# GpSimd makes the first tap of three convolved tiles and the rounding step of softplus; VectorE goes on from its results

## The chip, the core and the metric

The kernel runs on one core of a Trainium2 chip. The metric is the device time of one execution in microseconds (us); lower is better. The core has a matrix engine (TensorE, PE), VectorE (DVE), ScalarE (ACT), GpSimd (POOL) and SyncE (SP), which here only issues DMAs. Each engine runs its instructions in order, and semaphores order them between engines.

## What is computed

The reference normalises x (4 batches of 1024 tokens, 256 features), runs a stack of 8 Mamba layers on it, runs a mixture of experts on the same normalised input, and joins the two. The Mamba stack is where nearly all of the time goes. One layer, cut to what matters:

```
xin, z = split(x @ Wi.T)                          # 512 channels each
xin    = silu(causal_conv(xin, cw, cb))           # 4 taps a channel, plus a bias
dt_raw, Bm, Cm = split(xin @ Wx.T)                # 16, 16, 16
delta  = softplus(dt_raw @ Wdt.T + bdt)
h      = h * exp(delta * A) + (delta * xin) * Bm  # one h for each channel and each of 16 states
y      = sum over states of h * Cm, plus xin * Dp
x      = x + (y * silu(z)) @ Wo.T
```

## The kernel before

A *unit* is one layer, one batch and one half of its 1024 tokens: T = 512 tokens, 512 channels as 4 tiles of 128 channels (j = 0 to 3). There are 8 x 4 x 2 = 64 units (U), the two halves of a batch after each other: h = 0, then h = 1. Here a *plain* unit is one with h = 0, and a *carry* unit one with h = 1, whose scans start from the values that the half before left in `carry`. Units 2 to 61 run in a loop that holds a pair of them.

**One slot.** A unit has 64 slots, k = 4n + j, written (n, j): n is the state, j the channel tile. In slot k, POOL makes `drive` k = `du` times `brep`, which is delta times u times B (L884, two SBUF inputs of 128x512). ACT makes the decay `ps_d` = exp(delta * A) (L916), and DVE runs the recurrence over the 512 tokens as one scan (L1077). PE transposes the state (L1231), ACT weighs it by C (L923, `prod`), PE transposes it back and sums (L1238).

**How far each engine may run ahead.** POOL may be up to 8 slots ahead of the scans: `drive` has 8 places, and drive k waits for scan k - 8. ACT may be 2 ahead: `ps_d` has 2 places, and the decay of slot k + 2 is issued in ACT's slot k and waits for scan k. DMAs on SP's queue bring `brep` 4 states ahead.

**Work of the neighbouring units.** Between the slots of unit U the engines do the side work of U - 1, U + 1 and U + 2, at slots that hand-written tables name. What matters here:

- *The convolution* of unit U + 2 on DVE, tiles j = 0, 1, 2 (tile 3 is done by PE). `CONV_AT` lists 12 places, four taps for each tile; (n + 16, j) means (n, j) of the next unit. Tap 0 (L1114) is `xc = xpad * w + bias` and waits for ACT's copy of the tile into `xpad` (L929, ACT's slots (5,1), (9,0) and (11,0)); taps 1 to 3 (L1118) are `xc = xpad * w + xc`. Taps 0 and 1 of tile 0 both stand at (5,2); tap 0 of tile 1 at (9,2), of tile 2 at (15,1); the last tap at (3,0) of the next unit. POOL's `halo` at (3,2) (L863, L865) waits for that last tap before it overwrites the edge of `xpad`.
- *Softplus* of unit U + 1 on DVE, in two pairs of channel tiles p = 0, 1, at `SOFT_AT`. In `softplus`, part 0 (L1137) is the rounding step: `low` = (soft + 1) - 1. Part 1 (L1140) is `low = soft - low`, part 2 (L1144) adds the logarithm, part 3 (L1147) adds relu and finishes `delta`. For p = 0 the four parts stand at (7,3), (8,3), (9,3), (10,2), for p = 1 at (10,3), (11,3), (14,2), (14,3). Both pairs use the one tile `low`, so part 0 of p = 1 waits for part 3 of p = 0 (`delta_set`). Part 0 waits also for ACT's exponential (L985, ACT's slots (7,0) and (10,1)).
- *du* of unit U + 1 on DVE (L1127), two instructions behind part 3 at (14,3). The first waits until drive 61 of unit U is done, the second until drive 63 is, since they overwrite what these drives read:

```
dve.wait_ge(drive_set, TILES * F - 2 + 2 * p)
```

- *silu* on ACT at (4,2), with two table loads; *add* of the layer's output into `xres` on DVE at (4,3) and (6,1) (L1183); `gate` on DVE at (1,1) and (1,2) (L1177); the masked copy `xm` on POOL at (5,1) (L855); `carry` copies on POOL (L870), most of them in plain units, one behind every fourth drive.

Of the kernel before, what the change touches and what calls it, by code (L numbers as in the profile page):

```python
# [35 lines left out]
T = 512  # L36
# [619 lines left out]
def mamba(nc, w_in, w_x, w_dt, w_out, w_skip, w_conv, a_log, par, xres, ident, alive_dram, bc_dram, rate_dram):  # L656

    with ExitStack() as ctx:
# [48 lines left out]
        halo_set, conv_step, conv_done = sem("halo_set"), sem("conv_step"), sem("conv_done")  # L707
# [136 lines left out]
        def _(pool):  # L844
# [5 lines left out]
            def mask_x(U, kind, G, h, it):  # L850
                pool.wait_ge(ring_vec, item_read(U, kind, "CNT"))
                if not (isinstance(G, int) and G < 2):

                    pool.wait_ge(ring_ready, items_before(U, kind)[0])
                nc.gpsimd.tensor_tensor(xm[h][:], xres[:, :, bass.ds((it % BATCH) * SEQ + h * T, T)],  # L855
                                        alive[h][:].unsqueeze(1).to_broadcast([P, DB, T]), ALU.mult).then_inc(xm_set, 1)
# [10 lines left out]
            def keep_carry(U, n):  # L867

                wait_counted(scanned, TILES * U + CB * n + CB)
                nc.gpsimd.tensor_copy(carry[:, n, :], state[STATE_IN[n]][:, :, T - 1]).then_inc(carried, 1)  # L870

            def unit(U, h, it, kind):
                F, hf = U + 1, 1 - h
                G, itg = U + 2, it + 1
                for n in range(STATES):
                    for j in range(CB):
# [13 lines left out]
                        if kind != "last":  # L890
                            if (n, j) == HALO_AT:
                                halo(U, kind, F, hf)
                        if kind in ("first", "mid"):
                            if (n, j) == XM_AT:
                                mask_x(U, kind, G, h, itg)

            nc.gpsimd.memset(xdbl[:], 0.0).then_inc(xdbl_clear, 1)
            nc.gpsimd.memset(xpad[:, :, 0:TAPS - 1], 0.0).then_inc(halo_set, 1)
            mask_x(0, "pre0", 0, 0, 0)
            halo(0, "pre1", 0, 0)  # L900
            mask_x(0, "pre1", 1, 1, 0)
            units(pool, unit)

        @block.scalar
        def _(act):
# [111 lines left out]
            def unit(U, h, it, kind):  # L1017
                for n in range(STATES):
                    for t in range(TC):
                        k = CB * n + t + 2  # L1020
                        if k < TILES:
                            exponent(U, h, k)
                        elif kind != "last":
                            exponent(U + 1, 1 - h, k - TILES)
# [27 lines left out]
            exponent(0, 0, 0)  # L1052
            exponent(0, 0, 1)
# [5 lines left out]
        def _(dve):  # L1059
# [44 lines left out]
            def conv(copied, G, h, j, k):  # L1104

                tap = TAPS - 1 - k
                w = taps[h][:, j * TAPS + tap:j * TAPS + tap + 1]
                if k == 0:
                    dve.wait_ge(ring_act, copied)
                    if j == DVE_CONV[0]:  # L1110
                        dve.wait_ge(taps_in[h], loads_of(G, h))
                        if not is_first(G):
                            dve.wait_ge(u_set, G)
                    step = nc.vector.tensor_scalar(xc[:, j, :], xpad[:, j, tap:tap + T], w,  # L1114
                                                   taps[h][:, COL_CB + j:COL_CB + j + 1], ALU.mult, ALU.add)
                else:
                    dve.wait_ge(conv_step, (TAPS - 1) * (CV * G + DVE_CONV.index(j)) + k)
                    step = nc.vector.scalar_tensor_tensor(xc[:, j, :], xpad[:, j, tap:tap + T], w, xc[:, j, :], ALU.mult, ALU.add)  # L1118
                step.then_inc(conv_done if k == TAPS - 1 else conv_step, 1)
# [9 lines left out]
            def softplus(F, hf, p, part):  # L1129
# [19 lines left out]
            def early(U, h, kind, G, it, n, j):  # L1149

                for side in range(2):
                    if (n, j) == MARK_AT[side]:
                        mark_over(U, kind, G, h, it, side)
                if (n, j) == ALIVE_AT:
                    keep_alive(U, h, kind, G, h)
                for i in range(CV * TAPS):
                    if (n, j) == CONV_AT[i]:
                        conv(item_read(U, kind, f"X{DVE_CONV[i // TAPS]}"), G, h, DVE_CONV[i // TAPS], i % TAPS)

            def late(copied, F, hf, n, j):  # L1160

                for i in range(CV * TAPS):
                    if (n + STATES, j) == CONV_AT[i]:
                        conv(copied, F, hf, DVE_CONV[i // TAPS], i % TAPS)
                for i in range(8):
                    if (n, j) == SOFT_AT[i]:
                        softplus(F, hf, i // 4, i % 4)
# [17 lines left out]
            def unit(U, h, it, kind):  # L1185
                for n in range(STATES):
                    for j in range(CB):
# [6 lines left out]
                        if kind != "last":  # L1194
                            late(items_before(U, kind)[2], U + 1, 1 - h, n, j)
# [10 lines left out]
            for n in range(STATES):  # L1206
                for j in range(CB):
                    late(items_before(0, "pre1")[2], 0, 0, n, j)
# [326 lines left out]
```

## Time and profile before

| | |
|---|---|
| median of 3 runs | 7741.25 us (7739.77 to 7742.37) |
| the profiled execution, its own time | 7743.71 us |
| its span from first to last instruction | 7742.0 us |
| mean granted clock of TensorE | 0.987 |
| busy share of the span: PE, DVE, ACT, POOL | 90%, 86%, 83%, 77% |

The profile is one execution. Its page gives each engine's busy time and the costliest groups of instructions; the trace answers questions about a stretch, a tile or a line. The Mamba stack begins some 460 us into the span and runs to within some 50 us of its end. A pair of units takes about 225 us there, and one pair looks like the next almost to the tenth of a microsecond, so that the sum can be made over one pair (here the carry unit around 4026 to 4138 us and the plain unit behind it).

### The profile page before, as it was taken

What the parts mean: (1) busy time and instruction counts of PE and PEld (TensorE: products, weight loads), DVE (VectorE), ACT (ScalarE), POOL (GpSimd) and SP (SyncE); (2) the same over time, 40 slices, a digit from 0 to 9 for tenths busy, and PEclk for the clock granted to TensorE, in tenths of its full rate; (3) what the DMA queues carried; (4) which work ended last, traced back from release to release, by engine and by line L of the source; (5) the groups of instructions that cost most, each with busy time, mean ns of one, the idle gap of its engine ahead of it and who ended that gap; (6) DMA issues with size and microseconds to landing.
All of it is one profiled execution on the core that took longest, in us unless ns stands there. A gap on an engine that the chain in (4) does not pass through costs nothing. (4 is left out here: it accounts for less than half of the span.)

```text
span 7742.0 us, 143629 instructions
## 1 busy us (share of the span) xinstructions
PE 6941.3 (90%) x39999; PEld 4801.8 (62%) x39999; DVE 6668.0 (86%) x6510; ACT 6422.9 (83%) x10314; POOL 5929.2 (77%) x4917
## 2 busy tenths in 40 slices
PE   6979999999999999999999999999999999999997
PEld 4646666666666666666666666666666666666665
DVE  3259988988998899889889988988998898889888
ACT  1258888888888888888888888888888888888887
POOL 2148887888888888888888887888888788888875
PEclk9989999999999999999999999999999999999998
DMA  4111111111111111111111111111111111111112
GB/s 161 34 42 40 40 39 47 43 39 40 42 45 44 39 39 48 42 40 39 40 46 44 40 38 41 45 42 39 39 48 42 39 40 41 45 43 39 40 39 91
DMA packets 222613, 352.40 MB, mean 46 GB/s; under 512 B 43856, under 2 KB 78448, under 8 KB 221712
## 3 DMA queue, kind: packets, MB, share of 16 engines
q1 hardware_dynamic: 218048, 332.70, 14.6%
q0 software_dynamic: 3792, 10.38, 0.4%
q8 instruction: 365, 5.98, 0.3%
q14 instruction: 408, 3.34, 0.1%
HBM read 325.00 MB, written 17.98 MB: 44 GB/s over the span
## 5 line engine op out<-in xcount | busy, mean ns | idle before, releaser
L884 POOL TENSOR_TENSOR drive<-du,brep 128x512 f32<-128x512 f32 x4096 | 5505.9, 1374 | 708.3 <-DVE du L1127 385.6
L916 ACT ACTIVATE ps_d<-delta,cur 128x512 f32<-128x512 f32 x4096 | 2869.9, 701 | 373.9 <-DVE state L1077 354.8
L923 ACT ACTIVATE prod<-ps_r,cT 128x512 f32<-128x512 f32 x4096 | 2837.1, 693 | 245.4 <-PE ps_r L1231 243.9
L1231 PE MATMUL ps_r<-ident,state 128*128 128x128 f32 x16384 | 2564.0, 280 | 297.1 <-ACT prod L923 158.3
L1077 DVE TENSOR_TENSOR_SCAN state<-ps_d,carry,drive 128x512 f32<-128x512 f32 x2048 | 2517.7, 1266 | 260.6 <-ACT ps_d L916 258.5
L1077 DVE TENSOR_TENSOR_SCAN state<-ps_d,drive 128x512 f32<-128x512 f32 x2048 | 2396.8, 1206 | 245.6 <-ACT ps_d L916 233.0
L1238 PE MATMUL ps_y<-ident,prod 128*128 128x128 f32 x16384 | 2481.9, 276 | 25.9 <-ACT prod L923 25.9
L1238 PEld LDWEIGHTS ps_y<-ident,prod 128*128 128x128 f32 x16384 | 1938.9, 142 | 666.8 <-issue 499.4
L1231 PEld LDWEIGHTS ps_r<-ident,state 128*128 128x128 f32 x16384 | 1851.3, 142 | 729.9 <-ACT prod L923 462.5
L1278 PE MATMUL ps_r<-xm,w_inz_sb 128*128 128x512 f32 x1024 | 507.4, 618 | 81.6 <-ACT prod L923 81.6
L1270 PE MATMUL ps_r<-xm,w_inx_sb 128*128 128x512 f32 x1024 | 509.1, 620 | 21.9 <-ACT prod L923 14.2
L1318 PE MATMUL ps_r<-relu,w_out_sb 128*128 128x512 f32 x1024 | 473.9, 606 | 58.6 <-ACT prod L923 56.0
L1118 DVE SCALAR_TENSOR_TENSOR xc<-xpad,taps,xc 128x512 f32<-128x512 f32 x576 | 506.6, 880 | 2.6
L870 POOL COPY carry<-state 128x4 f32<-128x4 f32 x512 | 227.2, 444 | 222.2 <-DVE state L1077 222.1
L1311 PE MATMUL ps_r<-xdbl,w_dt_sb 16*128 16x512 f32 x512 | 295.0, 656 | 86.7 <-DVE xres L1183 52.1
L1318 PEld LDWEIGHTS ps_r<-relu,w_out_sb 128*128 128x128 f32 x1024 | 184.7, 190 | 272.8 <-issue 217.4
L1278 PEld LDWEIGHTS ps_r<-xm,w_inz_sb 128*128 128x128 f32 x1024 | 173.6, 189 | 260.4 <-ACT prod L923 126.7
L1270 PEld LDWEIGHTS ps_r<-xm,w_inx_sb 128*128 128x128 f32 x1024 | 175.1, 190 | 193.1 <-issue 149.3
L535 ACT ACTIVATE hid<-ps_t,b_sb 128x128 f32<-128x128 f32 x312 | 85.0, 383 | 227.4 <-PE ps_t L496 227.3
L1114 DVE TENSOR_SCALAR xc<-xpad,taps 128x512 f32<-128x512 f32 x192 | 189.2, 985 | 93.2 <-ACT xpad L929 93.2
L463 POOL DMA_INDIRECT ys_dram<-yb,row x39 | 37.5, 962 | 296.9 <-DVE yb L555 296.9
L1297 PE MATMUL ps_r<-u,w_x_sb 128*48 128x512 f32 x512 | 234.1, 601 | 33.3 <-ACT u L951 33.3
(144 smaller groups left out, 4647.3 us busy)
## 6 DMA issues: line engine op xcount, KB each, us to landing
brep<-bc_dram SPq DMA_DIRECT2D x1024, 256.0 KB, 3.2
w_sb<-w SPq DMA_DIRECT2D x8, 1024.0 KB
w_all<-w SPq DMA_DIRECT2D x8, 1024.0 KB, 11.4
xb<-xs_dram SPq DMA_DIRECT2D x39, 128.5 KB, 2.0
w_all<-x SPq DMA_DIRECT2D x4, 1024.0 KB, 9.1
w_inx_sb<-w_in SPq DMA_DIRECT2D x8, 512.0 KB, 4.1
w_inz_sb<-w_in SPq DMA_DIRECT2D x8, 512.0 KB, 4.5
w_out_sb<-w_out SPq DMA_DIRECT2D x8, 512.0 KB, 4.2
```

What stands on the lines that cost most here:

```text
L884: nc.gpsimd.tensor_tensor(drive[:, k % DRIVE, :], du[:, j, :], brep[:, n % BREP, :], ALU.mult).then_inc(drive_set, 1)
L916: nc.scalar.activation(ps_d[:, k % 2, :], delta[h][:, j, :], ACT.Exp, scale=cur[h][:, a:a + 1]).then_inc(decay_set, 1)
L923: nc.scalar.activation(prod[:, t, :], ps_r[:, item_place(U, h, kind, item), :], ACT.Copy, scale=cT[(h + 1) % 2 if item[1] == "prev" else h ...
L1077: nc.vector.tensor_tensor_scan(state[STATE_IN[n]][:, j, :], ps_d[:, k % 2, :], drive[:, k % DRIVE, :], carry[:, n, j:j + 1] if h == 1 else ...
L1118: step = nc.vector.scalar_tensor_tensor(xc[:, j, :], xpad[:, j, tap:tap + T], w, xc[:, j, :], ALU.mult, ALU.add)
L1231: last = nc.tensor.transpose(out[:, j * P:(j + 1) * P], state[STATE_IN[n]][:, j, t * P:(t + 1) * P], ident[:])
L1238: last = nc.tensor.matmul(ps_y[:, j, t * P:(t + 1) * P], prod[:, t, j * P:(j + 1) * P], ident[:], start=False, stop=True, is_transpose=Tru ...
L1270: last = nc.tensor.matmul(out, w_inx_sb[:, k, j * P:(j + 1) * P], xm[h][:, k, :], start=(k == 0), stop=(k == DB - 1))
L1278: last = nc.tensor.matmul(out, w_inz_sb[:, k, j * P:(j + 1) * P], xm[hf][:, k, :], start=(k == 0), stop=(k == DB - 1))
L1297: last = nc.tensor.matmul(out[0:XD, :], w_x_sb[:, k, :], u[:, k, :], start=(k == 0), stop=(k == CB - 1))
L1311: nc.tensor.matmul(out, w_dt_sb[:, j * P:(j + 1) * P], xdbl[0:RANK, :], start=True, stop=True).then_inc(ring_ready, 1)
L1318: last = nc.tensor.matmul(out, w_out_sb[:, j, k * P:(k + 1) * P], gated[:, j, :], start=(j == 0), stop=(j == CB - 1))
```

## The change

POOL takes over five instructions of each unit: tap 0 of tiles 0, 1 and 2 and part 0 of softplus for both pairs. The arithmetic and the tiles are the same. POOL issues them behind the drives of the slots in two new tables. `CONV_AT` and `SOFT_AT` stay as they are, with DVE leaving out tap 0 and part 0, so that DVE's tap 1 of tile 0 still stands at (5,2) while POOL's tap 0 stands at (6,1) of POOL's own order.

```diff
+TAP_AT, ROUND_AT = [(6, 1), (10, 1), (15, 2)], [(8, 2), (11, 2)]
...
+            def conv(copied, G, h, j):
+
+                wait_counted(ring_act, copied)
+                if j == DVE_CONV[0]:
+                    wait_counted(taps_in[h], loads_of(G, h))
+                    if not is_first(G):
+                        wait_counted(u_set, G)
+                nc.gpsimd.tensor_scalar(xc[:, j, :], xpad[:, j, TAPS - 1:TAPS - 1 + T], taps[h][:, j * TAPS + TAPS - 1:j * TAPS + TAPS],
+                                        taps[h][:, COL_CB + j:COL_CB + j + 1], ALU.mult, ALU.add).then_inc(conv_begun, 1)
+
+            def round_off(F, p):
+
+                wait_counted(exp_done, 2 * F + p + 1)
+                if p or not is_first(F):
+                    wait_counted(delta_set, 2 * F + p)
+                nc.gpsimd.tensor_scalar(low[:], soft[:, 2 * p:2 * p + 2, :], 1.0, 1.0, ALU.add, ALU.subtract).then_inc(soft_step, 1)
...
-            def conv(copied, G, h, j, k):
+            def conv(G, h, j, k):
...
-                if k == 0:
-                    dve.wait_ge(ring_act, copied)
...
-                    step = nc.vector.tensor_scalar(xc[:, j, :], xpad[:, j, tap:tap + T], w,
-                                                   taps[h][:, COL_CB + j:COL_CB + j + 1], ALU.mult, ALU.add)
+                if k == 1:
+                    dve.wait_ge(conv_begun, CV * G + DVE_CONV.index(j) + 1)
...
-                if part == 0:
-                    dve.wait_ge(exp_done, 2 * F + p + 1)
-                    if p or not is_first(F):
-                        dve.wait_ge(delta_set, 2 * F + p)
-                    nc.vector.tensor_scalar(low[:], soft[:, pair, :], 1.0, 1.0, ALU.add, ALU.subtract).then_inc(soft_step, 1)
```

The waits of `mask_x` on POOL become `wait_counted` (a wait and a semaphore increment, as the other POOL helpers have). The diff also brings two empty tables, `BOOST_AT` and `REST_AT`, and a table `DECAYS` made from them that lists the decays which ACT issues in each slot; with the tables empty it is the order of before.

## Rows read from the trace of the kernel before

**Rows 1.** The page: busy time of each engine.

```profile
PE 6941.3 (90%) x39999; PEld 4801.8 (62%) x39999; DVE 6668.0 (86%) x6510; ACT 6422.9 (83%) x10314; POOL 5929.2 (77%) x4917
```

**Rows 2.** Who waited for whom from 3000 to 5000 us: total, times, longest.

```profile
DVE state L1077 <- ACT ps_d L916: 138.3, 125, 3.6
POOL drive L884 <- DVE du L1127: 105.5, 18, 6.7
ACT ps_d L916 <- DVE state L1077: 98.1, 116, 2.2
```

**Rows 3.** Busy in windows (PE, PEld, DVE, ACT, POOL; clock): carry unit, plain unit, softplus stretch.

```profile
4026.85:4138.42 111.57, 101.69 (x585) 70.63 (x584) 100.72 (x95) 95.77 (x152) 88.54 (x69) 0.97 0.13 37
4138.42:4251.50 113.08, 102.59 (x603) 70.13 (x601) 101.00 (x95) 99.44 (x157) 92.97 (x80) 1.00 0.16 47
...
4050.00:4083.00 33.00, 30.44 (x192) 21.89 (x190) 32.18 (x31) 32.30 (x54) 30.65 (x20) 1.00 0.14 42
```

**Rows 4.** DVE around the first tap of tile 0: carry unit, then plain unit.

```profile
4029.98 2.10 DVE L1114 TENSOR_SCALAR xc<-xpad,taps 128x512 f32<-128x512 f32 x1 [1.05 <-ACT xpad L929]
...
4144.46 1.14 DVE L1114 TENSOR_SCALAR xc<-xpad,taps 128x512 f32<-128x512 f32 x1 [1.32 <-ACT xpad L929]
```

**Rows 5.** POOL and ACT in the same place of the carry unit.

```profile
4020.67 11.12 POOL L884 TENSOR_TENSOR drive<-du,brep 128x512 f32<-128x512 f32 x9
...
4029.25 0.60 ACT L929 ACTIVATE xpad<-ps_r 128x512 f32<-128x512 f32 x1 [0.46 <-PE ps_r L1270]
```

**Rows 6.** POOL's groups of instructions by shape over the whole span.

```profile
L855 POOL TENSOR_TENSOR xm<-xres,alive 128x1024 f32<-128x1024 f32 x64 | 151.3, 2364 | 9.8 <-DVE alive L1101 9.8
...
L897 POOL MEMSET xdbl<- 128x512 f32 x1 | 0.5, 525 | 5.3 <-POOLq L420 5.3
...
L190 POOL TENSOR_SCALAR_AFFINE_SELECT ident<-ident 128x128 f32<-128x128 f32 x1 | 0.3, 294 | 0.0
...
L186 POOL MEMSET ident<- 128x128 f32 x1 | 0.2, 205 | 0.0
```

**Rows 7.** DVE's other moved steps: round p = 0 and tap 0 of tile 1 (plain unit).

```profile
4161.92 1.05 DVE L1137 TENSOR_SCALAR low<-soft 128x1024 f32<-128x1024 f32 x1
...
4173.10 1.16 DVE L1114 TENSOR_SCALAR xc<-xpad,taps 128x512 f32<-128x512 f32 x1
```

**Rows 8.** DVE in the carry unit: part 3 of p = 0, round p = 1, du, tap 0 of tile 2.

```profile
4068.35 1.19 DVE L1147 TENSOR_TENSOR delta<-low,relu 128x1024 f32<-128x1024 f32 x1
...
4070.66 0.66 DVE L1137 TENSOR_SCALAR low<-soft 128x1024 f32<-128x1024 f32 x1
4071.24 1.27 DVE L1077 TENSOR_TENSOR_SCAN state<-ps_d,carry,drive 128x512 f32<-128x512 f32 x1
...
4095.26 2.35 DVE L1127 TENSOR_TENSOR du<-delta,u 128x1024 f32<-128x1024 f32 x2
...
4099.90 0.52 DVE L1114 TENSOR_SCALAR xc<-xpad,taps 128x512 f32<-128x512 f32 x1
```

**Rows 9.** DVE in the plain unit: part 3 of p = 0, and du.

```profile
4180.64 1.19 DVE L1147 TENSOR_TENSOR delta<-low,relu 128x1024 f32<-128x1024 f32 x1
...
4206.89 2.35 DVE L1127 TENSOR_TENSOR du<-delta,u 128x1024 f32<-128x1024 f32 x2
```

**Rows 10.** POOL: drives 47 to 63 (carry unit), drives of the plain unit, and the range of one.

```profile
4063.09 26.82 POOL L884 TENSOR_TENSOR drive<-du,brep 128x512 f32<-128x512 f32 x17 [0.19 <-DVE state L1077]
...
4195.71 4.97 POOL L884 TENSOR_TENSOR drive<-du,brep 128x512 f32<-128x512 f32 x4
...
4200.77 2.51 POOL L884 TENSOR_TENSOR drive<-du,brep 128x512 f32<-128x512 f32 x2
...
L884 POOL TENSOR_TENSOR drive<-du,brep x19: 1270/1292/2175, 4059.6 to 4088.6; 128x512 f32<-128x512 f32 x19
```

**Rows 11.** Windows: 30 us from tap 0 of tile 0 in two carry units.

```profile
4256.34:4286.34 30.00, 26.14 (x159) 18.02 (x157) 26.72 (x25) 25.80 (x43) 23.43 (x18) 1.00 0.12 39
4480.40:4510.40 30.00, 27.18 (x144) 18.83 (x143) 25.00 (x23) 24.25 (x40) 22.17 (x17) 0.89 0.12 36
```

More of the change, by code:

```diff
@@ L90 @@
 HALO_AT, XM_AT = (3, 2), (5, 1)
+LEAD = 2
 CONV_ITEMS = [f"C{j}" for j in PE_CONV]
+DECAYS, at = {}, LEAD
+for n, j in [(n, j) for n in range(STATES) for j in range(CB)]:
+    count = 1 + BOOST_AT.count((n, j)) - REST_AT.count((n, j))
+    DECAYS[n, j] = list(range(at, at + count))
+    at += count
 CV = CB - len(PE_CONV)
@@ L870, in keep_carry, with early, late @@
                 nc.gpsimd.tensor_copy(carry[:, n, :], state[STATE_IN[n]][:, :, T - 1]).then_inc(carried, 1)
+            def conv(copied, G, h, j):
[11 more added lines that the diff above has]
+                nc.gpsimd.tensor_scalar(low[:], soft[:, 2 * p:2 * p + 2, :], 1.0, 1.0, ALU.add, ALU.subtract).then_inc(soft_step, 1)
+            def early(U, h, kind, G, it, n, j):
+                for i in range(CV):
+                    if (n, j) == TAP_AT[i]:
+                        conv(item_read(U, kind, f"X{DVE_CONV[i]}"), G, h, DVE_CONV[i])
+            def late(copied, F, hf, n, j):
+                for i in range(CV):
+                    if (n + STATES, j) == TAP_AT[i]:
+                        conv(copied, F, hf, DVE_CONV[i])
+                for p in range(2):
+                    if (n, j) == ROUND_AT[p]:
+                        round_off(F, p)
             def unit(U, h, it, kind):
@@ L892, in unit @@
                                 halo(U, kind, F, hf)
+                            late(items_before(U, kind)[2], F, hf, n, j)
                         if kind in ("first", "mid"):
@@ L899, in _ @@
             mask_x(0, "pre0", 0, 0, 0)
+            for i in range(CV):
+                conv(item_read(0, "pre0", f"X{DVE_CONV[i]}"), 0, 0, DVE_CONV[i])
             halo(0, "pre1", 0, 0)
             mask_x(0, "pre1", 1, 1, 0)
+            for n in range(STATES):
+                for j in range(CB):
+                    for i in range(CV):
+                        if (n, j) == TAP_AT[i]:
+                            conv(item_read(0, "pre1", f"X{DVE_CONV[i]}"), 1, 1, DVE_CONV[i])
+                    for p in range(2):
+                        if (n, j) == ROUND_AT[p]:
+                            round_off(0, p)
             units(pool, unit)
@@ L1019, in unit @@
                     for t in range(TC):
[L1020 to L1024, printed above, removed]
+                        for k in DECAYS[n, t]:
+                            if k < TILES:
+                                exponent(U, h, k)
+                            elif kind != "last":
+                                exponent(U + 1, 1 - h, k - TILES)
                         if (n, t) == SILU_AT:
@@ L1051, in _ @@
                     early(0, 0, "pre1", 1, n, t)
-            exponent(0, 0, 0)
-            exponent(0, 0, 1)
+            for k in range(LEAD):
+                exponent(0, 0, k)
             units(act, unit)
@@ L1194, in unit @@
                         if kind != "last":
[L1195 removed]
+                            late(U + 1, 1 - h, n, j)
                         if kind in ("first", "mid"):
@@ L1207, in _ @@
                 for j in range(CB):
-                    late(items_before(0, "pre1")[2], 0, 0, n, j)
+                    late(0, 0, n, j)
                     early(0, 1, "pre1", 1, 0, n, j)
```

28 lines of the change are left out of this document (13 added, 15 removed).

## The prediction

> **What bounds the kernel now.** I read the page first: in busy time nobody is full, with PE at 90%, DVE at 86%, ACT at 83% and POOL at 77% [rows 1]. Then the waits of the stack. DVE loses most by waiting for ACT's decays (138.3 us in 2000), ACT nearly as much by waiting for DVE's scans (98.1), and POOL by waiting for `du` (105.5 in 18 waits, 5.9 each) [rows 2]. So the end is set by a chain that changes hands between DVE and ACT, two slots apart, while POOL sits beside it with slack. The windows say the same: in a pair of units DVE is busy 100.7 of 111.6 and 101.0 of 113.1 us, and in the softplus stretch both DVE (32.2 of 33) and ACT (32.3) are full [rows 3]. A microsecond taken from DVE is won where DVE holds the chain, and only in part where ACT is just as late.
>
> The sum is made over this pair, the time from a tap 0 to the same one two units on. It goes in 31 times (62 of the 64 units have a successor whose convolution is done between their slots, 63 a softplus). A dense instruction on DVE starts some 0.08 us before the row of the one before it ends, so removing it frees a little less than its row: for the round, 0.58 of 0.66 (from 4070.66 to 4071.24) [rows 8].
>
> **Tap 0 of tile 0.** DVE waits for ACT's copy, which ends at 4029.85 [rows 5], and starts 0.13 later. Its tap then takes 2.10 us in the carry unit and 1.14 in the plain one [rows 4]; tap 0 of tile 2 takes 0.52 [rows 8]. What is different is POOL: its nine drives run back to back from 4020.67 to 4031.79 [rows 5], and the tap ends just behind them. The tap and POOL's drives exclude each other here. The Trainium skill, "SBUF — State Buffer", section "Who interferes with whom", has the rule: the two engines share one pair of ports, and a `tensor_scalar` on DVE in a 2-port mode is wholly blocked while GpSimd holds it. The row agrees.
>
> After the change POOL stands behind drive 25 (done near 4025.6, the fourth of the nine), waits for the same copy and makes the tap itself, and DVE's tap 1 starts one hand-over (again 0.13) later. *Price of POOL's tap, P:* no row shows it. From below: a memset of 128x512 takes 0.525. From above: a drive, with two inputs, 1.27 undisturbed [rows 10]. Nearest is the affine_select, one input and arithmetic, 0.294 for 128 columns; with the memsets' 0.83 ns for each further column (0.525 less 0.205 over 384) it would be 0.61 for 512 and 1.04 for 1024 [rows 6]. Its own rate may be slower, and this form reads two scalars for each partition, so I take P = 0.70 and for the round R = 1.20; the ends are 0.53 and 1.27 for P, and 0.95 and 2.36 (`xm`, 128x1024 with two inputs) for R [rows 6]. Gain: 2.14 less 0.83 is 1.31 in the carry unit, 1.18 less 0.83 is 0.35 in the plain one. Behind it ACT waits for DVE's next scans, so this goes through.
>
> **Round p = 0 and tap 0 of tile 1.** Removed from DVE: in the carry unit 0.58 + 0.44, in the plain one 1.05 and 1.16, both again in POOL's way [rows 7]. But here ACT is full [rows 3]. Followed slot by slot (scan k no sooner than decay k, decay k + 2 no sooner than scan k and than ACT's line of work), DVE comes to part 3 of p = 0 earlier by 0.42 and by 1.10.
>
> **Round p = 1 and tap 0 of tile 2.** The first frees 0.58 in each unit. The second frees 0.44; ACT's decays are ready only some 0.3 before they are used there, so I count 0.30.
>
> Gross: 1.31 + 0.42 + 0.58 + 0.30 = 2.61 in the carry unit, 0.35 + 1.10 + 0.58 + 0.30 = 2.33 in the plain one, 4.94 a pair.
>
> **What the change adds: a chain through POOL.** Round p = 1 stands behind drive 46, and must wait for part 3 of p = 0, since both use `low`. In the carry unit that ends at 4069.54 [rows 8], while POOL was done with drive 46 before 4063.09 [rows 10]. So 6.45 us of its lead are gone, and behind the waiting round stand drives 47 to 63; DVE's second `du` waits for drive 63. Before, POOL was done 6.5 us before the second `du` starts in the carry unit (4089.91 against 4096.43) and 4.8 in the plain one (4203.28 against 4208.06) [rows 8 to 10]. This slack is the cover that POOL's new work was to have. From the end of part 3, in the carry unit:
> - POOL: hand-over 0.13, round 1.20, 17 drives at 1.235 (four take 4.97 with the last at its full 1.27 [rows 10], so they start 1.23 apart) 21.0, tap 0 of tile 2 behind drive 62 0.70. DVE's two-input steps hold up drives: the 17 of before took 26.8, 5.8 over the pure 21.0, for three 128x1024 steps, three taps and the round; I charge 0.9 for a 1024 step (1.27 to 2.17 [rows 10]) and 0.5 for a tap. Left are part 1 and two taps, 1.9, and, since POOL now still works then, parts 2 and 3 at 1.8 and the first `du`, 0.5. Sum 27.2.
> - DVE wants to start the second `du` at 4096.43 less 4069.54, 26.9, less the round 0.58: 26.3.
>
> So DVE waits some 0.9 there. In the plain unit DVE wants it at 4208.06 less 4181.83, 26.2, less 0.58, 25.65 [rows 9], and POOL has four carry copies at 0.15 more, 27.8: a wait of 2.15. Together 3.05, queued behind which are scans 60 to 63 and so ACT.
>
> Other waits are hidden: drive 47 is done 2.6 after part 3 (0.13 + 1.20 + 1.24), scan 47 starts about 4.9 after it. Round p = 0 waits for the exponential some 5 us, but scan 35 needs its drive 3 us later than POOL brings it. `halo` still waits for the last tap. `brep` is loaded four states ahead, its loads wait on drives long done.
>
> **The sum.** 4.94 less 3.05 is 1.9 a pair; 31 pairs, 59 us. The profiled execution took 7743.7 (span 7742.0 and 1.7 around it): 7685. The median of the runs is 2.5 below that execution: **7682 us**.
>
> **Rivals.**
> - *POOL's new instructions are as slow as its two-input ones* (slower than before). P = 1.24 and R = 2.36 add 0.54 at tap 0, and 0.54 + 1.16 to the chain into the second `du`, 2.24 a unit, 4.5 a pair: 1.9 becomes -2.6, +81 us, 7822. It decides from 0.95 a unit on, for example P = 0.95 with R = 1.65. For it: no two-scalar form of POOL is in the trace. Against it: the one-input rows are half as long [rows 6].
> - *More than I count, about 7590 or below.* If POOL keeps up with `du` (P and R at their lower ends, DVE's steps costing it less), 4.94 a pair stand, 153 us. And the blocked tap is followed by a stretch in which PE's granted clock falls from 2.4 to 1.2 GHz in some carry units: two carry units show a mean of 1.00 and 0.89 over the same 30 us [rows 11], and from tap to tap the pair of the 1.00 took 224.1 us (4256.34 to 4480.40) and the one of the sum, with 0.97 over its carry unit [rows 3], 226.4 (4029.98 to 4256.34). Half of that difference, since the drops differ from pair to pair, comes on top if they go: 1.1 a pair, 7555.
> - *Nothing is left.* If ACT takes all of the softplus gain (0.42 + 1.10 and 0.6 of the rounds p = 1), 2.8 less 3.05 remain, 7741 to 7750. The Trainium skill, "Perfetto Trace Analysis", section "Optimizing Scalar/DVE Operations", warns that offloading between VectorE and GpSimd "might not help", as they share a read port. Against this rival stands that the moved steps end POOL's exclusion of DVE at tap 0, which alone is 0.96 in the carry unit.
>
> **Chances and range.** Forecast (7640 to 7725) 0.50; more than that 0.17; nothing left 0.15; POOL too slow 0.18. The measurement can tell some 0.2%, 15 us, from no change. Faster is the first two, 0.67; same 0.14; slower 0.19. With a tenth left out on either side, the range goes to 7595 below and, since POOL's price is unknown up to 7822, to 7785 above. The likeliest case alone: 7640 to 7725.
>
> **What the profile after would show.** POOL's tap near 0.70 and round near 1.20. Tap 1 of tile 0 0.8 to 0.9 behind ACT's copy instead of 2.3 and 1.3. A new group of waits: DVE `du` on POOL `drive`, 1 to 2 us a unit, and POOL's wait for `du` nearly gone. DVE's busy time lower by some 4 us a pair and more. The prediction is wrong if P and R are off (it moves by 2 P + R a unit), if ACT holds more of the softplus stretch than I followed, or if drives are slowed more or less by DVE's two-input steps.

## The result and the profile after

The changed kernel takes **8274.81 us** (median of 4 runs, 8269.16 to 8289.14) against 7741.81 for the kernel before (4 runs): ratio 1.0692, 95% interval 1.0673 to 1.071. That is 533 us more, where 59 less were forecast. The sign was wrong, and the time lies far outside the range. The profiled execution took 8289.14 us (span 8287.4), at a mean granted clock of 0.963, where before had 0.987.

**Busy time** comes first, the page's row that answers to [rows 1]:

```profile
PE 7061.7 (85%) x39999; PEld 4944.2 (60%) x39999; DVE 6780.3 (82%) x6190; ACT 6451.8 (78%) x10314; POOL 6676.5 (81%) x5237
```

DVE has 320 instructions less and yet is busy 112 us longer; POOL has 320 more and is busy 747 us longer. Neither is full. So two things have to be found: why DVE's remaining work got longer, and who waits.

**POOL's groups after**, by line: count, busy us, mean ns, idle time before them and its releasers. L887 is the tap, L895 the round, L924 the drive.

```profile
L924 POOL TENSOR_TENSOR drive<-du,brep 128x512 f32<-128x512 f32 x4096 | 5588.4, 1396 | 73.3 <-DVE state L1129 56.1 <-DMA brep<-bc_dram 9.7 <-DVE du L1173 5.0
L895 POOL TENSOR_SCALAR low<-soft 128x1024 f32<-128x1024 f32 x128 | 465.5, 3637 | 173.4 <-ACT soft L1037 171.2 <-DVE delta L1188 2.1
...
L887 POOL TENSOR_SCALAR xc<-xpad,taps 128x512 f32<-128x512 f32 x192 | 197.6, 1029 | 299.8 <-ACT xpad L981 299.8
```

The round takes 3.64 us, three times what the sum took and half as much again as its upper end of 2.36. The tap, by contrast, has a median of 770 ns (757 to 2892) when its instances are listed, near the forecast 0.70; the mean is 1029 because some are held up. POOL's wait for `du`, behind which the prediction meant to hide POOL's new work, is gone: 5.0 us here; over the whole of before it was 385.6.

**DVE's groups after**, same view. L1164 is taps 1 to 3, L1181 and L1185 are parts 1 and 2 of softplus, L1173 is `du`.

```profile
L1129 DVE TENSOR_TENSOR_SCAN state<-ps_d,carry,drive 128x512 f32<-128x512 f32 x2048 | 2521.2, 1266 | 335.6 <-ACT ps_d L968 284.5 <-POOL drive L924 42.8 <-PE ps_r L1272 1.4
L1129 DVE TENSOR_TENSOR_SCAN state<-ps_d,drive 128x512 f32<-128x512 f32 x2048 | 2408.7, 1208 | 369.8 <-ACT ps_d L968 298.3 <-POOL drive L924 58.6 <-PE ps_r L1272 0.8
L1164 DVE SCALAR_TENSOR_TENSOR xc<-xpad,taps,xc 128x512 f32<-128x512 f32 x576 | 610.3, 1060 | 165.1 <-POOL xc L887 164.8
L1185 DVE TENSOR_TENSOR low<-low,delta 128x1024 f32<-128x1024 f32 x128 | 240.5, 1879 | 0.1
L1173 DVE TENSOR_TENSOR du<-delta,u 128x1024 f32<-128x1024 f32 x128 | 233.5, 1825 | 159.9 <-POOL drive L924 159.9
L1181 DVE TENSOR_TENSOR low<-soft,low 128x1024 f32<-128x1024 f32 x128 | 230.6, 1802 | 8.2 <-POOL low L895 8.2
```

And the same groups of the kernel before, so that the account can be drawn up:

```profile
L1077 DVE TENSOR_TENSOR_SCAN state<-ps_d,carry,drive 128x512 f32<-128x512 f32 x2048 | 2517.7, 1266 | 260.6 <-ACT ps_d L916 258.5 <-POOL drive L884 1.4 <-PE ps_r L1231 0.4
L1077 DVE TENSOR_TENSOR_SCAN state<-ps_d,drive 128x512 f32<-128x512 f32 x2048 | 2396.8, 1206 | 245.6 <-ACT ps_d L916 233.0 <-POOL carry L870 8.5 <-POOL drive L884 1.5
L1118 DVE SCALAR_TENSOR_TENSOR xc<-xpad,taps,xc 128x512 f32<-128x512 f32 x576 | 506.6, 880 | 2.6
L1114 DVE TENSOR_SCALAR xc<-xpad,taps 128x512 f32<-128x512 f32 x192 | 189.2, 985 | 93.2 <-ACT xpad L929 93.2
L1140 DVE TENSOR_TENSOR low<-soft,low 128x1024 f32<-128x1024 f32 x128 | 180.9, 1413 | 0.1
...
L1144 DVE TENSOR_TENSOR low<-low,delta 128x1024 f32<-128x1024 f32 x128 | 153.2, 1197 | 0.0
...
L1127 DVE TENSOR_TENSOR du<-delta,u 128x1024 f32<-128x1024 f32 x128 | 150.4, 1215 | 0.0
L1137 DVE TENSOR_SCALAR low<-soft 128x1024 f32<-128x1024 f32 x128 | 87.6, 685 | 1.2 <-ACT soft L985 1.1
```

| DVE, us over the run, after less before | |
|---|---|
| moved away: tap 0 (189.2) and rounds (87.6) | -276.8 |
| unchanged instructions that became longer: taps 1 to 3 +103.7, part 1 +49.7, part 2 +87.3, part 3 +1.3, `du` +83.1 | +325.1 |
| waits for POOL: tap 1 164.8 (for 93.2 of tap 0 on ACT), part 1 8.2, `du` 159.9, scans 101.4 (for 2.9) | +338.2 |
| scans' waits for ACT: 582.8 for 491.5 | +91.3 |
| together | +477.8 |

This is 478 of the span's 545; the rest lies in small groups. The second line is the surprise: 832 unchanged instructions (the 576 taps and 256 of the parts 1 and 2), and 128 `du`, take 324 us longer at the same shapes. The prediction had DVE's busy time fall by some 4 us a pair and more.

**What one pair shows.** The timeline of DVE in the carry unit, where the copy into `xpad` ended at 3094.55; the rows that answer to [rows 4] and [rows 8]. Columns: start, duration, and, in brackets, the idle time before it and what ended it.

```profile
3095.82 1.75 DVE L1164 SCALAR_TENSOR_TENSOR xc<-xpad,taps,xc 128x512 f32<-128x512 f32 x1 [2.20 <-POOL xc L887]
...
3125.31 1.89 DVE L1185 TENSOR_TENSOR low<-low,delta 128x1024 f32<-128x1024 f32 x1
...
3138.62 1.28 DVE L1129 TENSOR_TENSOR_SCAN state<-ps_d,carry,drive 128x512 f32<-128x512 f32 x1 [1.37 <-POOL drive L924]
3139.82 2.23 DVE L1181 TENSOR_TENSOR low<-soft,low 128x1024 f32<-128x1024 f32 x1
...
3160.97 1.21 DVE L1173 TENSOR_TENSOR du<-delta,u 128x1024 f32<-128x1024 f32 x1
3164.07 2.20 DVE L1173 TENSOR_TENSOR du<-delta,u 128x1024 f32<-128x1024 f32 x1 [1.90 <-POOL drive L924]
```

POOL in the same places:

```profile
3095.02 0.77 POOL L887 TENSOR_SCALAR xc<-xpad,taps 128x512 f32<-128x512 f32 x1 [4.69 <-ACT xpad L981]
3095.75 12.55 POOL L924 TENSOR_TENSOR drive<-du,brep 128x512 f32<-128x512 f32 x9
...
3124.86 1.27 POOL L924 TENSOR_TENSOR drive<-du,brep 128x512 f32<-128x512 f32 x1
...
3133.64 3.63 POOL L895 TENSOR_SCALAR low<-soft 128x1024 f32<-128x1024 f32 x1
3137.23 22.64 POOL L924 TENSOR_TENSOR drive<-du,brep 128x512 f32<-128x512 f32 x16
3159.86 2.89 POOL L887 TENSOR_SCALAR xc<-xpad,taps 128x512 f32<-128x512 f32 x1
```

And tap 1 in the kernel before:

```profile
4032.12 0.75 DVE L1118 SCALAR_TENSOR_TENSOR xc<-xpad,taps,xc 128x512 f32<-128x512 f32 x1
```

Read them together. Tap 1 starts at 3095.82, 1.27 after ACT's copy, 1.00 us sooner than in before (2.27 after the copy). The forecast was 1.31: POOL's tap starts 0.47 after the copy, where the sum had 0.13. And tap 1 starts 0.07 behind the start of POOL's next drive and lasts 1.75 instead of 0.75. It ends 3.02 after the copy; in before that was also 3.02. The gain at this place is wholly given back. In the plain unit (copy ends at 3213.73, tap 1 ends 3.13 later) it is a loss: before, 2.12. Part 2 at 3125.31 meets a drive that has 0.82 left (3124.86 + 1.27) and lasts 1.89; in before it never exceeded 1221 ns. The scan at 3138.62 waits for a drive that stands behind the round. The second `du` waits 1.90 for drive 63, which stands behind the 3.63 of the round and behind the tap at 3159.86. That tap takes 2.89 instead of 0.77: DVE's part 3 (3159.85) and first `du` (3160.97) run over it one after the other. Then the second `du` is itself stretched by the next unit's first drive.

Such a wait can reach PE. In the plain unit before, the second `du` waits 3.22 us (until 3041.98), and ACT behind it 6.18 us for a scan (until 3045.34). Windows of 5 us around it (busy PE, PEld, DVE, ACT, POOL; granted clock, DMA share, GB/s):

```profile
3035.00:3040.00 5.00, 5.00 (x29) 3.50 (x28) 3.75 (x4) 3.19 (x5) 5.00 (x4) 1.00 0.05 18
3040.00:3045.00 5.00, 1.63 (x7) 0.69 (x5) 3.02 (x2) 0.00 (x0) 5.00 (x4) 0.91 0.22 52
3045.00:3050.00 5.00, 3.31 (x16) 3.31 (x17) 4.32 (x5) 4.11 (x7) 5.00 (x6) 0.50 0.03 7
```

PE is busy for 1.63 of 5 us, and in the next 5 us its granted clock is 0.50 of full, 1.2 GHz. A rival of the prediction had such drops go away; over the whole span the mean granted clock fell from 0.987 to 0.963.

### The profile page after: what moved, and what is told of

It reads as the page before. It is cut to its first block and busy times, and to the rows that moved or that the text cites. A ratio compares the mean times of both kernels' runs of the same rounds, so it can differ in the third digit from the quotient of the medians.

```text
span 8287.4 us, 144226 instructions
## 1 busy us (share of the span) xinstructions
PE 7061.7 (85%) x39999; PEld 4944.2 (60%) x39999; DVE 6780.3 (82%) x6190; ACT 6451.8 (78%) x10314; POOL 6676.5 (81%) x5237
## 5 line engine op out<-in xcount | busy, mean ns | idle before, releaser
L924 POOL TENSOR_TENSOR drive<-du,brep 128x512 f32<-128x512 f32 x4096 | 5588.4, 1396 | 73.3 <-DVE state L1129 56.1
L1272 PE MATMUL ps_r<-ident,state 128*128 128x128 f32 x16384 | 2641.2, 286 | 692.8 <-ACT prod L975 466.6
L1272 PEld LDWEIGHTS ps_r<-ident,state 128*128 128x128 f32 x16384 | 1928.6, 146 | 1103.7 <-ACT prod L975 766.9
L1279 PE MATMUL ps_y<-ident,prod 128*128 128x128 f32 x16384 | 2550.6, 281 | 25.7 <-ACT prod L975 25.7
L1279 PEld LDWEIGHTS ps_y<-ident,prod 128*128 128x128 f32 x16384 | 2004.5, 146 | 668.0 <-issue 541.6
L1164 DVE SCALAR_TENSOR_TENSOR xc<-xpad,taps,xc 128x512 f32<-128x512 f32 x576 | 610.3, 1060 | 165.1 <-POOL xc L887 164.8
L895 POOL TENSOR_SCALAR low<-soft 128x1024 f32<-128x1024 f32 x128 | 465.5, 3637 | 173.4 <-ACT soft L1037 171.2
L887 POOL TENSOR_SCALAR xc<-xpad,taps 128x512 f32<-128x512 f32 x192 | 197.6, 1029 | 299.8 <-ACT xpad L981 299.8
L1173 DVE TENSOR_TENSOR du<-delta,u 128x1024 f32<-128x1024 f32 x128 | 233.5, 1825 | 159.9 <-POOL drive L924 159.9
```

Of the source, the lines that this page charges most:

```text
L895: nc.gpsimd.tensor_scalar(low[:], soft[:, 2 * p:2 * p + 2, :], 1.0, 1.0, ALU.add, ALU.subtract).then_inc(soft_step, 1)
L924: nc.gpsimd.tensor_tensor(drive[:, k % DRIVE, :], du[:, j, :], brep[:, n % BREP, :], ALU.mult).then_inc(drive_set, 1)
L1272: last = nc.tensor.transpose(out[:, j * P:(j + 1) * P], state[STATE_IN[n]][:, j, t * P:(t + 1) * P], ident[:])
L1279: last = nc.tensor.matmul(ps_y[:, j, t * P:(t + 1) * P], prod[:, t, j * P:(j + 1) * P], ident[:], start=False, stop=True, is_transpose=Tru ...
```

## The experiments

Times are medians, and differences are to runs of the kernel before made beside them on the same chip. Names used below: *theory A* holds that POOL's round form is slow and that this, through the chain into `du`, is the cause, so that the taps cost little; *rival B*, that POOL's new steps are slow only because DVE collides with them; *rival C*, that the taps alone cost much; *theory D* lays the taps' cost on POOL's lost lead, since a POOL without lead is busy whenever DVE's two-input steps come, and *rival E* on the tap work itself; *law L* is stated where it was formed, in experiment 5.

**1. What POOL's forms cost alone.** Before, with 24 POOL instructions ahead of the first drive, each waiting for the one before it, nothing else of POOL's changed.

```diff
+            for _ in range(2):
+                next_one(nc.gpsimd.tensor_scalar(out2, wide, 1.0, 1.0, ALU.add, ALU.subtract))
+                next_one(nc.gpsimd.tensor_scalar(out1, thin, 1.0, 1.0, ALU.add, ALU.subtract))
+                next_one(nc.gpsimd.tensor_scalar(out2, wide, 1.0, -1.0, ALU.add, ALU.add))
+                next_one(nc.gpsimd.tensor_scalar(out2, wide, 1.0, 1.0, ALU.mult, ALU.add))
+                next_one(nc.gpsimd.tensor_scalar(out1, thin, 1.0, 1.0, ALU.mult, ALU.add))
...
+                next_one(nc.gpsimd.tensor_scalar(out1, thin, one, one, ALU.mult, ALU.add))
...
+                next_one(nc.gpsimd.tensor_scalar(out2, wide, 1.0, None, ALU.add))
+                next_one(nc.gpsimd.tensor_tensor(out2, wide, drive[:, 2:4, :], ALU.subtract))
+                next_one(nc.gpsimd.tensor_copy(out2, wide))
```

> The kernel before, with 24 one-after-the-other instructions on POOL ahead of the first drive: twelve forms, each twice, with nothing of theirs shared with DVE (they add some 50 us and change nothing else). It asks what of the round's 3.64 us is its form. Theory A (the operations or the immediates make it slow): the round's form takes 3.64 here too, and at least one form of the same width (mult with add, or scalars from memory) takes about twice the tap's 0.77 less its fixed part, 1.3 to 1.5 us. Rival B (the round is slow in its place, held up by DVE and ACT beside it): the round's form takes 1.3 to 1.6 us here, as all forms of its width.

The single run took 7796.95 us, 54 more, about the work that was added. The timeline of POOL in the second round of the forms, in the order of the lines above (those left out answer to those left out there):

```profile
470.53 3.64 POOL L909 TENSOR_SCALAR drive<-drive 128x1024 f32<-128x1024 f32 x1
474.26 1.92 POOL L910 TENSOR_SCALAR drive<-drive 128x512 f32<-128x512 f32 x1
476.27 3.64 POOL L911 TENSOR_SCALAR drive<-drive 128x1024 f32<-128x1024 f32 x1
479.99 1.05 POOL L912 TENSOR_SCALAR drive<-drive 128x1024 f32<-128x1024 f32 x1
481.12 0.62 POOL L913 TENSOR_SCALAR drive<-drive 128x512 f32<-128x512 f32 x1
...
483.15 0.77 POOL L915 TENSOR_SCALAR drive<-drive 128x512 f32<-128x512 f32 x1
...
491.78 2.77 POOL L918 TENSOR_SCALAR drive<-drive 128x1024 f32<-128x1024 f32 x1
494.64 2.34 POOL L919 TENSOR_TENSOR drive<-drive 128x1024 f32<-128x1024 f32 x1
497.04 1.04 POOL L920 COPY drive<-drive 128x1024 f32<-128x1024 f32 x1
```

The form `(x + 1) - 1` takes 3.64 us undisturbed (the very first one in the run 4.18): theory A held here and rival B fell, though the fast forms are faster than theory A had them (1.05 and 1.20 for 1.3 to 1.5). The same shape as `x * 1 + 1` takes 1.05. Reading the scalars from memory adds 0.15 (0.77 for 0.62). So at one shape the time goes by the operations that are asked for, not by the number of inputs.

**2. The taps alone, and 3. the rounds alone.** Of the changed kernel, one half is given back to DVE each time.

```diff
-TAP_AT, ROUND_AT = [(6, 1), (10, 1), (15, 2)], [(8, 2), (11, 2)]
+TAP_AT, ROUND_AT = [(6, 1), (10, 1), (15, 2)], [(99, 0), (99, 0)]
...
-                    if (n, j) == SOFT_AT[i] and i % 4:
+                    if (n, j) == SOFT_AT[i]:
```

> The changed kernel with both rounds back on DVE in their old places; only the three first taps stay on POOL. Theory A (the slow round and the chain behind it cost nearly all): within 60 us of the kernel before, on either side, with no wait of du for drive. Rival C (POOL's taps cost as much by themselves, since DVE's two-input steps collide with a POOL that never rests): slower than before by 150 us or more.

7944.94 us, ratio 1.0262 (1.0245 to 1.0279), +202. Theory A's "within 60" fell, rival C held. With the tap's price as forecast and no round on POOL, the move is still a loss. DVE's part 2, from which nothing was taken, has a mean of 1885 ns against 1197.

```diff
-TAP_AT, ROUND_AT = [(6, 1), (10, 1), (15, 2)], [(8, 2), (11, 2)]
+TAP_AT, ROUND_AT = [(99, 1), (99, 1), (99, 2)], [(8, 2), (11, 2)]
...
+                if k == 0:
+                    dve.wait_ge(ring_act, copied)
```

> The changed kernel with the three first taps back on DVE in their old places; only the two rounds stay on POOL. Theory A: slower than the kernel before by 400 to 550 us of the 533, with the wait of du for drive still there at 1.5 to 3 us a unit. Rival C: slower by 350 us or less.

8109.55 us, ratio 1.0468 (1.045 to 1.0485), +367: between the two expectations. `du` waits 81.0 us for drives, 1.27 a unit, less than theory A's 1.5 to 3. The halves make 569 together, the whole 533, so they add up but for 36.

**4. POOL's wait for the copy, alone.** The kernel before, and POOL waits at (6, 1) for ACT's copy as the tap does, but does nothing there.

```diff
+                            if (n, j) == (6, 1):
+                                wait_counted(ring_act, item_read(U, kind, "X0"))
```

> The kernel before with one wait added: behind drive 25 (slot (6,1)), POOL waits until ACT has copied tile 0 of the convolution, as it does in the changed kernel ahead of its first tap. POOL makes no tap. Theory D (a POOL that has lost its lead of 8 slots no longer starts its drives when a scan ends, so DVE's two-input steps meet a drive under way and wait it out): slower by 80 to 200 us, DVE's part 2 of softplus for p = 0 at 1.5 us and more instead of 1.20. Rival E (the waiting itself is free, POOL's tap work is what costs): within 40 us of the kernel before.

7748.75 us, ratio 1.0007 (0.9997 to 1.0016). Theory D's charge for the lost lead fell: POOL waits 267.6 us at the new place and 197 less for scans (28.9 for 226.0), part 2 stays at a mean of 1197 ns, and the time does not move. POOL's wait for `du` stays too (385.4 for 385.6): by the end of a unit it has caught up. Taps 0 become shorter (mean 815 for 985 ns), taps 1 to 3 longer (982 for 880).

**5. Only tap 0 of tiles 1 and 2 on POOL.** These need no early wait, and cost POOL 1.54 us a unit.

```diff
-TAP_AT, ROUND_AT = [(6, 1), (10, 1), (15, 2)], [(8, 2), (11, 2)]
+TAP_AT, ROUND_AT = [(6, 1), (10, 1), (15, 2)], [(99, 0), (99, 0)]
...
-                for i in range(CV):
+                for i in range(1, CV):
                     if (n, j) == TAP_AT[i]:
```

> Only tap 0 of tiles 1 and 2 on POOL; tap 0 of tile 0 and both rounds on DVE. POOL has no wait at (6,1). Theory D: most of the 203 us of the three taps are gone, the time lies between 7700 and 7800. Rival E (two thirds of the tap work is still on POOL): slower than the kernel before by 100 us or more.

7859.45 us, ratio 1.0145 (1.0129 to 1.0162), +112: theory D fell, rival E held. Its timeline gave the law. DVE's parts 2 and 3 first, then POOL:

```profile
3126.99 2.04 DVE L1201 TENSOR_TENSOR low<-low,delta 128x1024 f32<-128x1024 f32 x1
...
3130.09 1.90 DVE L1204 TENSOR_TENSOR delta<-low,relu 128x1024 f32<-128x1024 f32 x1
```

```profile
3126.68 1.27 POOL L924 TENSOR_TENSOR drive<-du,brep 128x512 f32<-128x512 f32 x1
3127.93 1.74 POOL L887 TENSOR_SCALAR xc<-xpad,taps 128x512 f32<-128x512 f32 x1
3129.64 1.27 POOL L924 TENSOR_TENSOR drive<-du,brep 128x512 f32<-128x512 f32 x1
```

At 3126.99 the drive has 0.96 us left (to 3127.95): 1.19 + 0.96 less 0.1 is 2.05, measured 2.04. At 3130.09 it has 0.82 left: 1.91, measured 1.90. POOL's tap, started 0.94 into part 2, is stretched in its turn from 0.77 to 1.74. **Law L**: a DVE instruction with two SBUF inputs lasts its undisturbed time plus what is left, at its start, of the POOL instruction under way (less about 0.1); whatever POOL starts meanwhile waits for DVE's. The rows above obey it: part 2 at 3125.31, 1.19 + 0.82 - 0.1 = 1.91 for 1.89; tap 1 at 3095.82, 0.72 (the shortest such tap) + 1.20 - 0.1 = 1.82 for 1.75; `du` at most 2297 ns, which is 1.21 and nearly a whole drive. The Trainium skill, "SBUF — State Buffer", section "Who interferes with whom", states the same: against a GpSimd instruction that reads SBUF, a DVE one with two SBUF inputs contends, and whichever is first keeps the shared pair for its whole length. The traces agree, in both directions.

A few rows don't prove a law, so it was set against every tap 1 to 3, part 1 to 3 and `du` of each trace, 1088 a run, with the shortest of its kind as undisturbed time. It gives the duration within 0.08 us for all 1088 in the kernel before (434 of them met a POOL instruction), for all in edits 1, 4 and 8, for 973 in the changed kernel and 1054 in edit 6; over the twelve traces for 12605 of 13056. The exceptions are of two main kinds. In 358, POOL's instruction had begun less than 0.1 us before DVE's: DVE went first and was not stretched. In 68, DVE's step was passed over and waited out one to four further drives, as the longest tap of the changed kernel did, which began at 875.38, in the second of these four drives, and waited until the last had ended:

```profile
875.38 3.56 DVE L1164 SCALAR_TENSOR_TENSOR xc<-xpad,taps,xc 128x512 f32<-128x512 f32 x1
...
873.43 4.96 POOL L924 TENSOR_TENSOR drive<-du,brep 128x512 f32<-128x512 f32 x4
```

Tap 0, a `tensor_scalar` with one large input, is passed over as a rule in one place: in the carry units, tile 0, it takes 2.10 where the law gives 0.52 + 0.59 - 0.1 = 1.0, a whole drive more. Why it loses there twice, no run shows.

What the law says of the kernel before: part 2 of p = 0 began at 4062.93, when POOL was waiting for a scan (its next drive starts at 4063.09 [rows 10]), and part 2, part 3 and the first `du` behind it at a time when POOL was done with drive 63 at 4089.91 and had none under way [rows 8, 10]. Parts 2, 3 and `du` have means of 1196 to 1215 ns there, and part 2 never passes 1221. By the law, POOL's waits were why they were fast.

```profile
4062.93 1.20 DVE L1144 TENSOR_TENSOR low<-low,delta 128x1024 f32<-128x1024 f32 x1
```

**6. All five moved, with the fast form.** `low` becomes `soft * 1 + 1` on POOL; DVE's part 1 makes `(low - 1) - soft`, part 2 subtracts it. The arithmetic's roundings are the same, the number of instructions too.

```diff
-                nc.gpsimd.tensor_scalar(low[:], soft[:, 2 * p:2 * p + 2, :], 1.0, 1.0, ALU.add, ALU.subtract).then_inc(soft_step, 1)
+                nc.gpsimd.tensor_scalar(low[:], soft[:, 2 * p:2 * p + 2, :], 1.0, 1.0, ALU.mult, ALU.add).then_inc(soft_step, 1)
...
-                    nc.vector.tensor_tensor(low[:], soft[:, pair, :], low[:], ALU.subtract).then_inc(soft_step, 1)
+                    nc.vector.scalar_tensor_tensor(low[:], low[:], 1.0, soft[:, pair, :], ALU.subtract, ALU.subtract).then_inc(soft_step, 1)
```

> The changed kernel with another form of the rounding: POOL makes low = soft * 1 + 1 (1.05 us alone instead of 3.64), DVE's part 1 is (low - 1) - soft in one step, part 2 subtracts it. The arithmetic and the result are the same. With R = 1.05 and P = 0.77 the sum of the prediction gives about 7680. Theory D: the slow round is gone but POOL's lost lead is not, so it stays at 7930 to 8050, DVE's two-input steps still longer than before. If the prediction failed by R alone: 7640 to 7740.

7946.49 us, ratio 1.0266 (1.0249 to 1.0283), +199. This is the prediction's own case: tap 0.77, round 1.05 (forecast 0.70 and 1.20). Its sum gives about 7680 with them. The account by R alone (7640 to 7740) fell; the time lies in theory D's range, though edit 4 had taken its mechanism away. The two groups of its DVE that got most:

```profile
L1164 DVE SCALAR_TENSOR_TENSOR xc<-xpad,taps,xc 128x512 f32<-128x512 f32 x576 | 586.1, 1018 | 166.3 <-POOL xc L887 166.0
L1185 DVE TENSOR_TENSOR low<-delta,low 128x1024 f32<-128x1024 f32 x128 | 255.4, 1995 | 0.8 <-ACT delta L1041 0.8
```

No `du` waits for POOL any more (mean 1212, no idle time), so the forecast chain is gone altogether. But taps 1 to 3 cost 79.5 us more than in before, part 1 39.8, part 2 102.2, part 3 40.3, together 262 of the 277 that the moves took from DVE; tap 1 waits 72.8 more for POOL than tap 0 did for ACT, and the scans 76.1 more for ACT. So DVE is busy for 38 us more than in before (6706.0 for 6668.0), with 320 instructions less, and these two waits come on top.

**7. The fast rounds alone.** Edit 6 with the taps of edit 3.

> The same fast rounding on POOL, with all taps on DVE as before. Theory D: POOL waits at (8,2) for the exponential and at (11,2) for part 3 and loses its lead there, so slower than the kernel before by 40 to 180 us, against 367 with the slow form. If only the length of the round mattered: 7700 to 7745.

7853.73 us, ratio 1.0144 (1.0127 to 1.0161), +106, for 2.1 us of POOL work a unit. The account by the round's length alone fell. The time is in theory D's range again, but parts 1 and 2 with means of 1620 and 1466 ns are what law L asks for too. The slow form against the fast one, rounds alone: 256 us.

**8. POOL held back in the kernel before.** If POOL's drives cost DVE time at tap 0, keeping POOL still there should gain. POOL waits behind drive 25 until DVE has finished taps 0 and 1 of tile 0; nothing is moved.

```diff
+                            if (n, j) == (6, 1):
+                                wait_counted(conv_step, CV * (TAPS - 1) * G + 2)
```

> The kernel before (all taps and rounds on DVE), with POOL held behind drive 25 until DVE has finished taps 0 and 1 of tile 0. Law L (a DVE step that needs the shared ports lasts its undisturbed time plus what is left of the POOL instruction under way): tap 0 takes 0.52 instead of 2.10 and 1.14, tap 1 keeps its 0.75, 2.2 us a pair, up to 68 us faster, 7680 to 7725 after some of it goes to ACT and to POOL's lost lead. Theory D (lost lead as such costs): slower by 30 us or more.

**7679.16 us**, ratio 0.9913 (0.9899 to 0.9926), 65 us faster than the kernel before and faster than either version. DVE at tap 0 of tile 0, where [rows 4] had 2.10:

```profile
4003.68 0.55 DVE L1116 TENSOR_SCALAR xc<-xpad,taps 128x512 f32<-128x512 f32 x1 [1.05 <-ACT xpad L931]
4004.27 0.75 DVE L1120 SCALAR_TENSOR_TENSOR xc<-xpad,taps,xc 128x512 f32<-128x512 f32 x1
```

Theory D's loss did not come. POOL waits 359.8 us at that place over the run, which delays nobody by more than it gives. Edit 4 held POOL only until the copy had landed, so it set off with the tap; this one lets both taps pass. That 65 is so near the law's 68 is in part luck: the law's 68 is the saving at tap 0 of tile 0, but taps 1 to 3 became 20 us longer and the rounds 12, so that DVE's busy time fell by 22 us only, while the scans waited 34 us less for ACT and the mean granted clock rose to 0.993.

**9. The same hold in edit 6.** POOL waits behind its first tap until DVE's tap 1 is done.

```diff
+                            if (n, j) == TAP_AT[0]:
+                                wait_counted(conv_step, CV * (TAPS - 2) * G + 1)
```

> The kernel of e6 (all five steps on POOL, fast rounding) with POOL held behind its first tap until DVE has finished tap 1 of tile 0. Law L: tap 1 takes 0.75 instead of 1.75, 1.0 us a unit, 40 to 65 us less than e6's 7946. Rival: POOL is the bound there and holding it costs, no gain or slower than e6.

7858.62 us, ratio 1.0146 (1.013 to 1.0161), 88 us less than edit 6 and more than the law's estimate. A loss of 115 remains, and part 2 still has a mean of 2037 ns: only one of the places was cleared.

**10. POOL work that nobody waits for more.** The kernel before, with drives 34 and 46 made twice: some 2.5 us of POOL work a unit, no step of DVE's removed, no new wait on another engine (POOL waits for its own first copy of the drive).

```diff
+                        if (n, j) in ((8, 2), (11, 2)):
+                            nc.gpsimd.tensor_tensor(drive[:, k % DRIVE, :], du[:, j, :], brep[:, n % BREP, :], ALU.mult).then_inc(again, 1)
+                            wait_counted(again, 2 * U + 1 + ((n, j) == (11, 2)))
```

> The kernel before, with POOL making drives 34 and 46 twice (the second time into the same place): 2.5 us more of POOL's work a unit, with no new wait on another engine and none of DVE's work taken away. By the prediction's count (POOL's end 6.5 and 4.8 us ahead of du covers it): within 20 us of the kernel before. Law L (POOL's idle tail is what kept parts 2 and 3 of softplus undisturbed on DVE): slower by 60 to 140 us, with parts 2 and 3 at 1.35 to 1.7 us instead of 1.20.

7794.73 us, ratio 1.0064 (1.0049 to 1.008), +51: the prediction's "within 20" fell, and the law's 60 to 140 was too high. Its DVE groups of softplus:

```profile
L1143 DVE TENSOR_TENSOR low<-soft,low 128x1024 f32<-128x1024 f32 x128 | 208.2, 1626 | 0.1
...
L1147 DVE TENSOR_TENSOR low<-low,delta 128x1024 f32<-128x1024 f32 x128 | 180.2, 1408 | 0.0
```

Part 1 is 27.3 us longer over the run and part 2 27.0, together 54, and the time 51. By the prediction's way of counting this work was hidden: `du` waits for nobody (mean 1213, no idle time before it). POOL's extra work alone costs, through DVE's steps. But the expectation named the wrong steps: part 3 stays at 1198 ns, and part 1 was not named. What got longer is part 1 of p = 1 in the carry units (2.1 for 1.2 us), far from the end of the unit, and part 2 of p = 1 in the plain ones (2.0 for 1.2), where POOL had been done only 0.24 before it (4203.28 against 4203.52). In the carry units POOL is done as far ahead of part 2 as before, since it waits less for scans (179 us before drives over the run, for 226).

## Why the prediction was wrong

**The step "Price of POOL's round, R = 1.20", ends 0.95 and 2.36.** It measured 3.64, outside both. The upper end came from `xm`, a row with two inputs, as if one input could not be dearer. It can: on POOL, add then subtract costs 3.5 times multiply then add. Changing only the form (edit 6) takes 328 us off the changed kernel. The prediction said that no two-scalar form of POOL was in the trace, and had a rival for a slow POOL; by its rule of 2P + R a unit, 2.44 more for R is 4.9 a pair, 151 us. The measured 328 is twice that. With both measured prices the prediction's own sum gives 7842, so the prices alone leave 433 of the measured time unexplained. For the price P (forecast 0.70, measured 0.77) the step was right. The Trainium skill, "GPSIMD Engine Reference", section "Engine selection", calls one-input work on GpSimd roughly line-rate; here multiply, add with 1.05 takes 1.6 times DVE's 0.66 for the round of the same shape, and add, subtract with 3.64 takes 5.5 times as long. For that pair of operations the measurement goes against the page.

**The step "DVE's two-input steps hold up drives; I charge 0.9 for a 1024 step and 0.5 for a tap".** This is the deeper failure, as edit 6 shows: with R and P as forecast the kernel is at 7946, 266 above the sum's 7680. The exclusion was seen at tap 0, with its row and its rule, and then charged to one side only. DVE's parts 1, 2, 3, `du` and taps 1 to 3 were left at their durations of before, though those of parts 2, 3 and `du` came from a POOL that stood still just then (part 1 and the taps were already stretched a little: means of 1413 for 1199 and 880 for 718 ns). In edit 6 parts 1 to 3 and taps 1 to 3 take 262 us more, a term that the sum had at nothing. It is of the size of the gap of 266, but the two are not a balance: some of it may be hidden behind ACT, and other waits come and go (below). The same oversight lies in "DVE's tap 1 starts one hand-over later, gain 1.31": it starts 1.00 sooner than before, and runs 1.0 longer, as it meets the drive that POOL starts just before it. The prediction also put the exclusion at tap 0 at 0.96, which is only the carry unit's tap less the plain one's; against the undisturbed 0.52 it is 1.58 and 0.62.

**The step "this slack is the cover that POOL's new work was to have".** The slack was there (6.5 and 4.8 us), and in the changed kernel it was used up, as forecast. But the chain into `du` was priced too high: with R = 3.64 the step gives 3.05 + 4.9 = 7.9 a pair, and 5.0 came (159.9 us over the run); with R and P as forecast (edit 6) it gives 3.05, 95 us over the run, and none came. So the forecast sum was held down by a wait that wasn't there, and what it left out is larger than the gap of 266 shows. And the slack wasn't free: by the law, POOL's standing still kept parts 2, 3 and `du` at 1.2 us. Edit 10 prices some of it: 2.5 us of POOL work a unit, nowhere waited for, costs 0.8 us a unit.

**What was right.** Tap 1 did start sooner after the copy (1.27 for 2.27, with 0.8 to 0.9 forecast), POOL's wait for `du` did go, and in the changed kernel a wait of `du` for a drive came. Rival "POOL as slow as two-input" had the sign but 7822 for 8275; it had R too small still, and counted tap 0 and the chain only.

**What stays open.** How far each collision's cost depends on where in POOL's rhythm DVE begins: the drives (1.235 apart) and the scans (1.19) run nearly in step, so one moved instruction shifts many later meetings. The law explains single instructions; which of them meet was not predicted by any run, and the estimates of edits 9 and 10 missed by 23 and 9 us. How much of the 533 comes from PE's clock (0.963 for 0.987) was not separated. Stretched steps cost without it, though: edits 5, 9 and 10 lost 112, 115 and 51 us at mean granted clocks of 0.987 to 0.991, where the runs of the kernel before had 0.984 to 0.987.

## What to carry to other kernels

Before moving elementwise work to GpSimd, list the instructions of VectorE that need the shared access (here those with two SBUF inputs, and the `tensor_scalar` of tap 0) in the stretch where GpSimd will now be busy, and charge each with what may be left of a GpSimd instruction, up to a whole one (in edit 6, part 2 lost 0.80 us on average and a tap 0.14); GpSimd's idle time there is cover for VectorE, not free capacity. Price a GpSimd instruction by a run of that very pair of operations, not by its inputs, and see whether `x * 1 + c` can stand in for `(x + a) - b`. Where VectorE stands on the critical path and meets a run of GpSimd instructions that has slack, one wait that keeps GpSimd still for two instructions can gain (here 0.9%) with nothing moved.

## What the hardware showed that was not expected

- GpSimd's `tensor_scalar` on 128x1024: 3.64 us for add, subtract and for add, add; 2.77 for a single add; 1.05 for multiply, add; 1.04 for a copy. A two-input subtract takes 2.34, so a one-input add is dearer than a two-input subtract.
- For these forms of GpSimd, scalars from memory instead of immediates cost 0.15 us more, at 512 and at 1024 columns (0.62 to 0.77, 1.05 to 1.20; 3.64 to 3.79).
- A VectorE step that waits for GpSimd can be passed over by further GpSimd instructions: in edits 2, 5, 6 and 9 some taps take 5.8 us instead of 0.72, with five drives back to back.
- The shortest instance of part 1 on DVE is 1199 ns in the kernel before, in edit 6 and, within 1 ns, in edit 7, though in the last two it does two operations instead of one.
- Moving the 128 rounds in their fast form (1.05 us each on POOL) makes the run 106 us longer, though it takes 87.6 us of work from DVE and makes no `du` wait for a drive.
